# Loading Wk in quarters, two x tiles between the halves of Wq, and two blocks of Wq turned later, in a fused graph-network kernel

## The chip, the cores and the metric

One core of one Trainium2 chip runs the whole program. The metric is the device time of one execution in microseconds, taken as the median of the runs. The kernel before takes 307.28 us (three runs, all 307.28).

## What is computed

Two layers over a graph of N = 1024 nodes with D = 512 features and 16384 edges (src, dst), with dst sorted:

```
h = relu(layernorm(x))
q = h @ Wq + bq;  k = h @ Wk + bk;  v = h @ Wv + bv
a = q @ k.T / sqrt(512), masked to the pairs that are edges
x = x + softmax(a) @ v
h = relu(layernorm(x))
# degree-normalised aggregation with self loops, twice, with a batch norm and relu between
x = x + agg(relu(bn(agg(h @ W1 + b1))) @ W2 + b2)
```

The scores are not made from q and k apart. They are h (Wq Wk^T) h^T plus bias terms, so a matrix M = Wq Wk^T is made first. For it both weights are turned (transposed) on TensorE. The adjacency is a matrix of edge counts that TensorE sums up from one-hot matrices, which VectorE builds. Every float32 product is made as three passes over a high and a low part.

## The kernel before, in words

All engines run orders written out by hand and meet at semaphores. Nothing is planned at run time, so the order of the work is the order of the code.

The opening has these steps. ScalarE's queue issues the load of Wk in two halves (line 429). SyncE's queue issues the edge lists, the two halves of Wq (line 263), four tiles of x (line 243), and the two halves of Wv (line 259). TensorE first runs 26 small products on zeros.

An *item* is one block that goes through three engines: TensorE fills a bank of PSUM (`make`), ScalarE evicts the high part (`hi_of`, line 491), and VectorE subtracts it to get the low part (`lo_of`, line 688). The kinds that matter here:

- ("t", K, c) and ("t", Q, c): block c (128 rows, 256 KB) of Wk or Wq is turned with four transposes (line 1023). Below they are K0 to K3 and Q0 to Q3.
- ("m", n, 0), below m0 to m3: block n of M, twelve matmul passes (lines 989 to 991). m_n reads turned block n of Wq as its stationary side, and **all four** turned blocks of Wk.
- ("h", n, 0): a tile of normalised x is turned, and ("v", n, 0) is its product with Wv.

`start` gives each early item its bank. `nth(item)` is the item's number in the order of the list. The semaphores item_ps, item_hi and item_lo count items, so a wait for item_lo at nth(item) means that all items up to that one are done.

TensorE's order before is K0, K1, two transposes of the edge lists (bank 3), K2, K3, Q0, Q1, Q2, Q3, m0, one small transpose of `lim` into bank 0 (line 1085), m1, m2, the edge counts of window 0 (line 1055), m3, counts of window 1, h0 to h3, v0, v1, counts of window 2, and so on. m0 waits until the low part of Q0 is written, m1 for Q1, m2 for Q2 and m3 for Q3.

VectorE's order before is lo(K0), lo(K1), copies of the edge columns (lines 755 and 756, `ecol_ready`), lo(K2), lo(K3), lo(Q0), lo(Q1), `limits()` (seven small steps, lines 654 to 662, ending in `lim_ready`), lo(Q2), the read of the turned `lim` (line 762, `bounds_ready`), a load of a bound into a register, lo(Q3), `onehots(0)` (lines 705 and 707), the next bound, the low part of half of Wv (line 673), `onehots(1)`, and so on. The ring of one-hots has four places, so VectorE can be at most four groups ahead of TensorE.

ScalarE's order before is hi of K0 to Q3, `stats(0)` (sums of x tiles 0 and 1), hi(m0), half of Wv, `stats(2)`, hi(m1) and so on.

Of the kernel before, what the change touches and what calls it, by code (L numbers as in the profile page):

```python
# [17 lines left out]
P = 128  # L18
# [4 lines left out]
KC = D // P  # L23
NCH = E // P
HALF = 512
WIN = 64
NW = N // WIN
# [9 lines left out]
LOADS = 2  # L37
WARM = 26
XT = 4
# [19 lines left out]
def gnn_kernel(nc, x, src, dst, Wq, bq, Wk, bk, Wv, bv, W1, b1, gamma, beta, W2, b2, out):  # L59
# [14 lines left out]
    def hold(name, kib):  # L74
# [86 lines left out]
    ident_zeroed ident_ready zeros_ready pad_ready iota_ready tables_ready consts  # L161
    dst_in src_in ext_ready ext_ps edge_f_ready ecol_ps ecol_ready drel_ready lim_ready lim_ps bounds_ready
    x_in0 x_in1 x_in2 x_in3 qk_bias_in bcol_in bias_in b1_in
    Wk_in0 Wk_in1 Wq_in0 Wq_in1 wB_in0 wB_in1 w2_in0 w2_in1 w_hi w_lo
    x_sums x_means x_squares ln_scale ln_coef h_ready item_ps item_hi item_lo uw_ready hw_second fill_ready
    ncol_ready lead_cols lead_dist lead_made onehots onehots_used c_done c16 loops_added adj_in0 adj_in1 adj_in2 adj_in3
    deg_ready degm_ready degm_ps flag_ready dinv_ready
# [8 lines left out]


    K, Q = 0, 1
    start = {("t", K, 0): 4, ("t", K, 1): 5, ("t", K, 2): 6, ("t", K, 3): 7, ("t", Q, 0): 2, ("t", Q, 1): 3,
             ("t", Q, 2): 4, ("t", Q, 3): 5, ("m", 0, 0): 6, ("m", 1, 0): 7, ("m", 2, 0): 2, ("m", 3, 0): 3,  # L180
             ("h", 0, 0): 4, ("h", 1, 0): 5, ("h", 2, 0): 6, ("h", 3, 0): 7}
    ahead = [[], [], [("v", 0, 0), ("v", 1, 0)], [("v", 2, 0), ("h", 4, 0)], [("v", 3, 0), ("h", 5, 0)],
# [2 lines left out]
    final = {("q", 1, c): 4 + c for c in range(KC)}  # L185
    items = list(start) + sum(ahead, []) + list(final)
    nth = lambda item: items.index(item) + 1
    item_bank = lambda item: start.get(item, final.get(item, 2 + (items.index(item) - len(start)) % ITEM_BANKS))
    last_in = lambda b, end: max([n for n, other in enumerate(items[:end], 1) if item_bank(other) == b] + [0])

# [41 lines left out]
    @block.sync  # L232
    def _(sp):

        sp.dma_start(edge_i[:, 0, :], dst.rearrange("(c j) -> c j", j=P)).then_inc(S["dst_in"], 16)
        sp.dma_start(edge_i[:, 1, :], src.rearrange("(c j) -> c j", j=P)).then_inc(S["src_in"], 16)

        def load_x(n):
            if XT <= n < NT + XT:
                sp.wait_ge(S["h_ready"], n - XT + 1)  # L240
            if n >= NT + XT:
                sp.wait_ge(S["x1_ready"], n - NT - XT + 1)
            sp.dma_start(xt[:, n % XT, :], x[(n % NT) * P:(n % NT + 1) * P, :]).then_inc(S[f"x_in{n % XT}"], 16)

        def turn_counts(t):

            if t == 0:
                sp.wait_ge(S["c16"], 2 * NW)
            if t >= ADJ:
                sp.wait_ge(S["masked"], t - ADJ + 1)  # L250
            sp.dma_start_transpose(adj[:, t % ADJ, :].rearrange("p (b n) -> p b n", b=NT),
                                   cnt16[:, t, :, :].rearrange("p b n -> p (b n)")).then_inc(
                S[f"adj_in{t % ADJ}"], 16)

        def load_w(i):

            k = KC // LOADS
            for j in range(LOADS):
                sp.dma_start(weight_load(i, j, "raw"), weights[i][0].rearrange("(k p) n -> p k n", p=P)[
                    :, j * k:(j + 1) * k, :]).then_inc(S[f"{weights[i][3]}{j}"], 16)  # L260

        for j in range(LOADS):
            sp.dma_start(half_of_qk(Q, j), half_in_dram(Wq, j)).then_inc(S[f"Wq_in{j}"], 16)
        for t in range(XT):
            load_x(t)
        load_w(0)
        for t in range(XT, NT):
            load_x(t)
        for i, b in ((K, bq), (Q, bk)):
            sp.dma_start(bias_row[:, i, :], b.rearrange("(o n) -> o n", o=1).to_broadcast([P, D])).then_inc(S["qk_bias_in"], 16)  # L270
        for i, b in enumerate((gamma, beta)):
            sp.dma_start(bcol[:, i, :], b.rearrange("(c p) -> p c", p=P),
                         allow_slow_non_contiguous=True).then_inc(S["bcol_in"], 16)
        for t in range(XT):
            load_x(NT + t)
        sp.wait_ge(S["item_ps"], nth(("v", NT - 1, 0)))
        load_w(1)
        sp.wait_ge(S["uw_ready"], 4)
        sp.dma_start(bias_row[:, 0, :], bv.rearrange("(o n) -> o n", o=1).to_broadcast([P, D])).then_inc(S["bias_in"], 16)
        sp.dma_start(bias_row[:, 1, :], b1.rearrange("(o n) -> o n", o=1).to_broadcast([P, D])).then_inc(S["b1_in"], 16)  # L280
        def turn_p(t, part, split, done, landed):

            sp.wait_ge(S[split], t + 1)
            if t >= 1:
                sp.wait_ge(S[done], t)
            sp.dma_start_transpose(p16T[:, part, :, :], p16[:, part, :]).then_inc(S[landed], 16)

        def turn_h2(t, part, split, done, landed):

            sp.wait_ge(S[split], t + 1)  # L290
            if t >= 1:
                sp.wait_ge(S[done], t)
            sp.dma_start_transpose(h16T[:, part, :, :], h16[:, part, :]).then_inc(S[landed], 16)

        for t in range(ADJ):
            turn_counts(t)
        for t in range(NT + 1):
            if t < NT:
                turn_p(t, 0, "p16_hi", "p_hi", "p16_hi_in")
                turn_p(t, 1, "p16_lo", "p_lo", "p16_lo_in")  # L300
            if XT <= t + 3 < NT:
                load_x(NT + t + 3)
            if t == 0:
                load_w(2)
            if t + ADJ < NT:
                turn_counts(t + ADJ)
            if t >= 1:
                turn_h2(t - 1, 0, "h16_hi", "h2T_hi", "h16_hi_in")
                turn_h2(t - 1, 1, "h16_lo", "h2T_lo", "h16_lo_in")
        sp.wait_ge(S["xb_ready"], NT)  # L310
        sp.dma_start(bias_row[:, 0, :], b2.rearrange("(o n) -> o n", o=1).to_broadcast([P, D])).then_inc(S["bias_in"], 16)
        for t in range(NT):
            sp.wait_ge(S["out_ready"], t + 1)
            sp.dma_start(out[t * P:(t + 1) * P, :], xt[:, t % XT, :]).then_inc(S[f"out_done{t % XT}"], 16)
        for u in range(XT):
            sp.wait_ge(S[f"out_done{u}"], 16 * NT // XT)
# [108 lines left out]

    @block.scalar
    def _(act):
        for j in range(LOADS):
            act.dma_start(half_of_qk(K, j), half_in_dram(Wk, j)).then_inc(S[f"Wk_in{j}"], 16)

        def split_w(i, loads=range(LOADS)):

# [5 lines left out]
        def stats(t):  # L438

            if t == KC:  # L440
                act.wait_ge(S["item_ps"], nth(("m", KC - 1, 0)))
            for u in (t, t + 1):
                act.wait_ge(S[f"x_in{u % XT}"], 16 * (u // XT + 1))
                act.activation(row_of(u), xt[:, u % XT, :], ACT.Copy, accum_out=xsum[:, 0, u:u + 1]).then_inc(S["x_sums"], 1)
            act.wait_ge(S["x_sums"], t + 2)
            act.activation(lnc[:, 0, t:t + 2], xsum[:, 0, t:t + 2], ACT.Copy, scale=-1.0 / D).then_inc(S["x_means"], 2)
            act.wait_ge(S["x_means"], t + 2)
            for u in (t, t + 1):
                act.activation(row_of(u), xt[:, u % XT, :], ACT.Square, bias=lnc[:, 0, u:u + 1],
                               accum_out=xsum[:, 1, u:u + 1]).then_inc(S["x_squares"], 1)  # L450
# [28 lines left out]
        def hi_of(item):  # L479

            what, n, c = item
            act.wait_ge(S["item_ps"], nth(item))
            if what == "q":
                if item == ("q", 0, 0):
                    act.wait_ge(S["uw_ready"], 4)
# [12 lines left out]
            act.activation(T[:, t % 2, :], zerob[:, 0:1].to_broadcast([P, N]), ACT.Identity,  # L498
                           bias=fill[:, t:t + 1]).then_inc(S["mask_set"], 1)

        for item in list(start)[:8]:
            hi_of(item)
        stats(0)
        hi_of(("m", 0, 0))
        split_w(0, (0,))
        stats(2)
# [121 lines left out]
    def _(dve):  # L628
# [67 lines left out]
        def bounds_of(i):  # L696
            return dve.value_load(lohi[0:1, ORDER[i]:ORDER[i] + 1], min_val=256, max_val=257 * NCH)
# [59 lines left out]
        for item in early[2:6]:  # L757
            lo_of(item)
        limits()
        lo_of(early[6])  # L760
        dve.wait_ge(S["lim_ps"], 1)
        dve.tensor_scalar(lohi[0:1, :], bank(0)[0:1, 0:NW], float(NCH), None, ALU.add).then_inc(S["bounds_ready"], 1)
        dve.wait_ge(S["bounds_ready"], 1)
        bounds = bounds_of(0)
        lo_of(early[7])
        dve.wait_ge(S["ecol_ready"], 2)
        onehots(0, bounds)
        bounds = bounds_of(1)
        split_w(0, 0)
        onehots(1, bounds)  # L770
        bounds = bounds_of(2)
# [214 lines left out]
    def _(pe):  # L986
# [18 lines left out]
        def make(item):  # L1005
# [4 lines left out]
            if what in "htw":  # L1010
                if what == "h":
                    pe.wait_ge(S["h_ready"], n + 1)
                elif what == "t":
                    pe.wait_ge(S[f"{'Wk' if n == K else 'Wq'}_in{c // 2}"], 16)
                    if item_bank(item) == 3:
                        pe.wait_ge(S["ecol_ready"], 2)
                else:
                    pe.wait_ge(S["uw_ready"], 4)
                for k in range(KC):
# [59 lines left out]
        for a in range(2):  # L1079
            m = pe.transpose(bank(3)[:, a * P:(a + 1) * P], edge_f[:, a, :], ident[:, :])  # L1080
        m.then_inc(S["ecol_ps"], 1)
        for item in early[2:9]:
            make(item)
        pe.wait_ge(S["lim_ready"], 1)
        pe.transpose(bank(0)[:, 0:P], lim[:, 4:5].to_broadcast([P, P]), ident[:, :]).then_inc(S["lim_ps"], 1)
        for item in early[9:11]:
            make(item)
        pe.wait_ge(S["consts"], 1)
        pe.wait_ge(S["bounds_ready"], 1)
# [186 lines left out]
```

## Time and profile before

| | us |
|---|---|
| median of the runs | 307.28 |
| the profiled execution | 307.32 |
| its span | 305.5 |
| TensorE busy (matmul) | 295.5 (97%) |
| VectorE busy | 207.0 (68%) |
| ScalarE busy | 159.9 (52%) |

The span is what the profile covers; 1.8 us of the execution's time lie around it. The stretch that the change touches is the first 20 us. There the transposes of the weights, their evictions, the loads and the small steps on the edge lists run side by side. In the timeline each line gives a start, a length, the engine, the line of the kernel, the tile written and the tiles read, and in brackets how long the engine had been idle and who ended that.

### The profile page before, as it was taken

What the parts mean: (1) busy time and instruction counts of PE and PEld (TensorE: products, weight loads), DVE (VectorE), ACT (ScalarE), POOL (GpSimd) and SP (SyncE); (2) the same over time, 40 slices, a digit from 0 to 9 for tenths busy, and PEclk for the clock granted to TensorE, in tenths of its full rate; (3) what the DMA queues carried; (4) which work ended last, traced back from release to release, by engine and by line L of the source; (5) the groups of instructions that cost most, each with busy time, mean ns of one, the idle gap of its engine ahead of it and who ended that gap; (6) DMA issues with size and microseconds to landing.
All of it is one profiled execution on the core that took longest, in us unless ns stands there. A gap on an engine that the chain in (4) does not pass through costs nothing.

```text
span 305.5 us, 4845 instructions
## 1 busy us (share of the span) xinstructions
PE 295.5 (97%) x1345; PEld 227.3 (74%) x1345; DVE 207.0 (68%) x458; ACT 159.9 (52%) x266; POOL 57.6 (19%) x103
## 2 busy tenths in 40 slices
PE   7999889899999999999999999999999999999995
PEld 6777356466665888888888888887888888878884
DVE  3899999999977557965748575568344388276311
ACT  3999967989546546445444544357523044342000
POOL 5361353000000530032131420203010044100000
PEclk9999999999999999999999999999999999999999
DMA  7806040000600309444362625313102000000321
GB/s 256 311 23 186 1 141 0 1 0 2 207 0 3 69 3 238 79 95 89 85 148 43 150 40 104 67 38 69 34 20 52 0 3 0 0 2 0 111 98 69
DMA packets 42312, 21.67 MB, mean 71 GB/s; under 512 B 35760, under 2 KB 36016, under 8 KB 42288
## 3 DMA queue, kind: packets, MB, share of 16 engines
q1 hardware_dynamic: 41744, 20.33, 26.0%
q10 hardware_dynamic: 544, 1.05, 0.9%
q8 instruction: 12, 0.20, 0.3%
q14 instruction: 12, 0.10, 0.1%
HBM read 10.88 MB, written 2.10 MB: 42 GB/s over the span
## 4 chain that ended last, share of the span: by engine, by line
PE 86%; DVE 7%; issue 2%; DMA 1%; DVEq 1%; ACT 1%; ACTq 0%
PE ps L989 20%; PE ps L991 19%; PE ps L990 19%; PE ps L1242 10%; PE ps L1165 8%; PE ps L1055 8%; DVE src_oh L705 2%; DMA qk_raw<-L_gnn_Wk_in 1%; PE ps L1023 1%; DVE dst_oh L707 1%; DVEq L705 1%; DVE WT L688 1%; DVE T L809 0%; DVE smx L813 0%; DVE p L821 0%
## 5 line engine op out<-in xcount | busy, mean ns | idle before, releaser
L705 DVE TENSOR_SCALAR src_oh<-iota,ecol 128x512 f16 x135 | 40.0, 349 | 3.0 <-PE ps L1055 2.5
L1055 PE MATMUL ps<-src_oh,dst_oh 128*128 x135 | 34.0, 382 | 3.7 <-DVE dst_oh L707 3.3
L1165 PE MATMUL ps<-cnt,qh 128*128 128x512 f32 x128 | 30.1, 391 | 0.3 <-ACT cnt L575 0.3
L1055 PEld LDWEIGHTS ps<-src_oh,dst_oh 128*128 x135 | 13.3, 103 | 21.9 <-issue 12.5
L1242 PE MATMUL ps<-qh,cnt 128*128 128x512 f32 x128 | 29.3, 390 | 0.0
L1165 PEld LDWEIGHTS ps<-cnt,qh 128*128 128x128 f32 x128 | 23.9, 188 | 5.6 <-DVE qh L868 0.7
L1242 PEld LDWEIGHTS ps<-qh,cnt 128*128 128x128 f32 x128 | 24.0, 188 | 5.3 <-DVE vb L970 0.3
L991 PE MATMUL ps<-v,pT 128*128 128x512 f32 x64 | 25.0, 390 | 0.0
L989 PE MATMUL ps<-v,pT 128*128 128x512 f32 x64 | 24.9, 389 | 0.0
L989 PE MATMUL ps<-hT,qh 128*128 128x512 f32 x64 | 24.9, 389 | 0.0
L990 PE MATMUL ps<-v,pT 128*128 128x512 f32 x64 | 24.9, 389 | 0.0
L990 PE MATMUL ps<-hT,qh 128*128 128x512 f32 x64 | 24.9, 389 | 0.0
L991 PE MATMUL ps<-hT,qh 128*128 128x512 f32 x64 | 24.9, 389 | 0.0
L403 POOL TENSOR_SCALAR lnb<-bnag 128x1 f32<-128x1 f32 x8 | 7.2, 898 | 81.6 <-DVE bnag L842 81.6
L464 ACT ACTIVATE cnt<-ps 64x512 int16<-64x512 f32 x32 | 18.9, 590 | 6.0 <-PE ps L1072 5.4
L982 DVE SCALAR_TENSOR_TENSOR xt<-ps,dinv,x 128x512 f32<-128x512 f32 x8 | 5.7, 747 | 17.1 <-PE ps L1242 17.1
L531 ACT ACTIVATE T<-T,smx 128x1024 f32<-128x1024 f32 x8 | 9.2, 1154 | 13.9 <-DVE smx L814 13.9
L831 DVE TENSOR_SCALAR pT<-p16T 128x1024 fp32r<-128x1024 f16 x8 | 5.5, 693 | 15.6 <-DMA p16T<-p 15.5
L559 ACT ACTIVATE hnT<-h16T 128x512 fp32r<-128x512 f16 x8 | 5.1, 632 | 20.2 <-DMA h16T<-h 20.2
L809 DVE COPY_PREDICATED T<-adj,ps 128x1024 f32<-128x1024 int16 x8 | 10.6, 1321 | 7.4 <-PE ps L991 7.4
L498 ACT ACTIVATE T<-zerob,fill 128x1024 f32<-128x1024 bf16 x8 | 9.1, 1146 | 12.4 <-DVE p L821 12.4
L707 DVE TENSOR_TENSOR dst_oh<-iota_w,drel_first 128x384 f16 (+1 forms) x35 | 14.7, 421 | 0.6 <-PE ps L1055 0.6
(186 smaller groups left out, 685.2 us busy)
## 6 DMA issues: line engine op xcount, KB each, us to landing
xt<-x_in SPq DMA_DIRECT2D x16, 256.0 KB, 3.3
out<-xt SPq DMA_DIRECT2D x8, 256.0 KB, 2.1
qk_raw<-L_gnn_Wk_in ACTq DMA_DIRECT2D x2, 512.0 KB, 5.0
qk_raw<-L_gnn_Wq_in SPq DMA_DIRECT2D x2, 512.0 KB, 6.8
wB_raw<-L_gnn_Wv_in SPq DMA_DIRECT2D x2, 512.0 KB, 9.0
wB_raw<-L_gnn_W_in SPq DMA_DIRECT2D x2, 512.0 KB, 4.1
w_raw<-L_gnn_W_in SPq DMA_DIRECT2D x2, 512.0 KB, 4.6
bias_row<-L_gnn_b_in SPq DMA_DIRECT2D x2, 256.0 KB, 4.7
```

The source lines that it names most:

```text
L464: act.activation(cnt16[rows, a * KC:(a + 1) * KC, w // 2, :], ps[a * WIN:(a + 1) * WIN, i % 2, :].rearrange("p (s n) -> p s n", n=P), ACT. ...
L498: act.activation(T[:, t % 2, :], zerob[:, 0:1].to_broadcast([P, N]), ACT.Identity, bias=fill[:, t:t + 1]).then_inc(S["mask_set"], 1)
L531: act.activation(T[:, t % 2, :], T[:, t % 2, :], ACT.Exp, bias=smx[:, 1, t:t + 1], scale=SCALE, accum_out=smx[:, 2, t:t + 1]).then_inc(S[" ...
L705: dve.tensor_scalar(src_oh[:, bass.ds(slot, 1), j, :].rearrange("p a n -> p (a n)"), iota[:, :], ecol[:, bass.ds(c + j, 1)], None, ALU.is_ ...
L707: dve.tensor_tensor(dst_oh[:, bass.ds(slot, 1), :, 0:count].rearrange("p a n u -> p (a n) u"), iota_w[:, :, 0:count], drel(i)[:, bass.ds(c ...
L809: dve.copy_predicated(T[:, t % 2, :], adj[:, t % ADJ, :], ps[:, 2 * (t % 2):2 * (t % 2) + 2, :].rearrange("p a n -> p (a n)")).then_inc(S[ ...
L989: pe.matmul(out_, stat(1), mov(0), start=first, stop=False)
L990: pe.matmul(out_, stat(0), mov(1), start=False, stop=False)
L991: return pe.matmul(out_, stat(0), mov(0), start=False, stop=last)
L1055: m = pe.matmul(ps[:, i % 2, :], dst_oh[:, bass.ds(slot, 1), :, j].rearrange("p a n -> p (a n)"), lead_oh[:, i % 2, j, :] if first and ACT ...
L1165: m = pe.matmul(bank(g), qh[:, d, a, c * P:(c + 1) * P], cnt[:, d, n * HALF:(n + 1) * HALF], start=(d == 0 and a == 1), stop=last)
L1242: m = pe.matmul(bank(t), cnt[:, d, t * P:(t + 1) * P], qh[:, d, a, :], start=(d == 0 and a == 1), stop=last)
```

## The change

Wk is loaded as four quarters, one for each block, and each has a semaphore of its own. On SyncE's queue x tiles 0 and 1 are now issued behind the first half of Wq, and x tiles 2 and 3 behind the second half. Q1 gets bank 0 in place of bank 3, and the turned `lim` gets bank 3 in place of bank 0. TensorE now makes m0 behind Q1, then turns `lim`, then Q2 and Q3, then m1. ScalarE does `stats(0)` before hi(Q2) and hi(Q3). VectorE does `onehots(0)` and loads the next bound before lo(Q2) and lo(Q3). `nth_made` is the number of an item in TensorE's new order, and ScalarE's waits use it.

```diff
-    start = {("t", K, 0): 4, ("t", K, 1): 5, ("t", K, 2): 6, ("t", K, 3): 7, ("t", Q, 0): 2, ("t", Q, 1): 3,
+    start = {("t", K, 0): 4, ("t", K, 1): 5, ("t", K, 2): 6, ("t", K, 3): 7, ("t", Q, 0): 2, ("t", Q, 1): 0,
+    in_order_made = items[:6] + items[8:9] + items[6:8] + items[9:]
+    nth_made = lambda item: in_order_made.index(item) + 1
@@ sync
         for j in range(LOADS):
             sp.dma_start(half_of_qk(Q, j), half_in_dram(Wq, j)).then_inc(S[f"Wq_in{j}"], 16)
-        for t in range(XT):
-            load_x(t)
+            for t in range(2 * j, 2 * j + 2):
+                load_x(t)
@@ scalar
-        for j in range(LOADS):
-            act.dma_start(half_of_qk(K, j), half_in_dram(Wk, j)).then_inc(S[f"Wk_in{j}"], 16)
+        for c in range(KC):
+            act.dma_start(qk_raw[:, K, c, :], Wk[c * P:(c + 1) * P, :]).then_inc(S[f"Wk_in{c}"], 16)
-        for item in list(start)[:8]:
+        for item in list(start)[:6]:
             hi_of(item)
         stats(0)
+        for item in list(start)[6:8]:
+            hi_of(item)
         hi_of(("m", 0, 0))
@@ vector
         limits()
-        lo_of(early[6])
         dve.wait_ge(S["lim_ps"], 1)
-        dve.tensor_scalar(lohi[0:1, :], bank(0)[0:1, 0:NW], float(NCH), None, ALU.add).then_inc(S["bounds_ready"], 1)
+        dve.tensor_scalar(lohi[0:1, :], bank(3)[0:1, 0:NW], float(NCH), None, ALU.add).then_inc(S["bounds_ready"], 1)
         dve.wait_ge(S["bounds_ready"], 1)
         bounds = bounds_of(0)
-        lo_of(early[7])
         dve.wait_ge(S["ecol_ready"], 2)
         onehots(0, bounds)
         bounds = bounds_of(1)
+        for item in early[6:8]:
+            lo_of(item)
         split_w(0, 0)
@@ tensor
-                    pe.wait_ge(S[f"{'Wk' if n == K else 'Wq'}_in{c // 2}"], 16)
-                    if item_bank(item) == 3:
-                        pe.wait_ge(S["ecol_ready"], 2)
+                    pe.wait_ge(S[f"Wk_in{c}" if n == K else f"Wq_in{c // 2}"], 16)
-        for item in early[2:9]:
+        for item in early[2:6] + early[8:9]:
             make(item)
+        pe.wait_ge(S["ecol_ready"], 2)
         pe.wait_ge(S["lim_ready"], 1)
-        pe.transpose(bank(0)[:, 0:P], lim[:, 4:5].to_broadcast([P, P]), ident[:, :]).then_inc(S["lim_ps"], 1)
-        for item in early[9:11]:
+        pe.transpose(bank(3)[:, 0:P], lim[:, 4:5].to_broadcast([P, P]), ident[:, :]).then_inc(S["lim_ps"], 1)
+        for item in early[6:8] + early[9:11]:
             make(item)
```

## Rows read from the trace of the kernel before

**Rows 1.** The page: shares of the chain that ended last, by engine.

```profile
PE 86%; DVE 7%; issue 2%; DMA 1%; DVEq 1%; ACT 1%; ACTq 0%
```

**Rows 2.** Timeline, TensorE, 8 to 19 us: start, length, engine, line, tiles, count.

```profile
8.04 1.09 PE L1023 MATMUL ps<-ident,qk_raw 128*128 128x128 f32 x8 [0.19 <-DMA qk_raw<-L_gnn_Wq_in]
...
9.48 1.07 PE L1023 MATMUL ps<-ident,qk_raw 128*128 128x128 f32 x8 [0.34 <-DVE WT L688]
...
10.30 0.48 PE L989 MATMUL ps<-WT 128*128 128x512 f32 x1
...
13.14 0.27 PE L1085 MATMUL ps<-ident,lim 128*128 128x128 f32 x1
...
13.16 0.48 PE L989 MATMUL ps<-WT 128*128 128x512 f32 x1
...
15.99 0.39 PE L989 MATMUL ps<-WT 128*128 128x512 f32 x1
...
18.72 1.26 PE L1055 MATMUL ps<-src_oh,dst_oh 128*128 x5
```

**Rows 3.** Timeline, ScalarE and VectorE, 8 to 18 us, same columns.

```profile
8.19 2.47 DVE L688 TENSOR_TENSOR WT<-ps,WT 128x512 fp32r<-128x512 f32 x4
...
8.73 1.09 ACT L491 ACTIVATE WT<-ps 128x512 fp32r<-128x512 f32 x2 [0.20 <-PE ps L1023]
...
10.59 0.34 DVE L654 TENSOR_SCALAR hit<-ps,win 128x128 f32<-128x128 f32 x1
...
13.44 0.16 DVE L762 TENSOR_SCALAR lohi<-ps 1x16 int32<-1x16 f32 x1
...
14.56 0.69 DVE L688 TENSOR_TENSOR WT<-ps,WT 128x512 fp32r<-128x512 f32 x1 [0.95 <-DVE lohi L762]
...
15.16 0.60 DVE L705 TENSOR_SCALAR src_oh<-iota,ecol 128x512 f16 x2
...
17.42 1.23 DVE L673 TENSOR_TENSOR wB<-wB_raw,wB 128x1024 fp32r<-128x1024 f32 x1 [0.20 <-issue]
```

**Rows 4.** Timeline: the issues of the loads on both queues.

```profile
0.72 0.98 ACTq L429 DMA_DIRECT2D qk_raw<-L_gnn_Wk_in  x2
...
1.65 0.94 SPq L263 DMA_DIRECT2D qk_raw<-L_gnn_Wq_in  x2
...
2.63 2.12 SPq L243 DMA_DIRECT2D xt<-x_in  x4
```

**Rows 5.** DMA view, short windows: each load, KB, us from issue to landing.

```profile
qk_raw<-L_gnn_Wk_in ACTq DMA_DIRECT2D x1, 512.0 KB, 4.4
...
qk_raw<-L_gnn_Wk_in ACTq DMA_DIRECT2D x1, 512.0 KB, 5.5
qk_raw<-L_gnn_Wq_in SPq DMA_DIRECT2D x1, 512.0 KB, 6.3
edge_i<-src_in SPq DMA_DIRECT2D x1, 64.0 KB, 4.1
...
qk_raw<-L_gnn_Wq_in SPq DMA_DIRECT2D x1, 512.0 KB, 7.2
xt<-x_in SPq DMA_DIRECT2D x1, 256.0 KB, 7.4
```

**Rows 6.** DMA view, 4.5 to 5.0 us: queue, packets, MB, share (q10 ScalarE's, q1 SyncE's).

```profile
q10 hardware_dynamic: 91, 0.18, 92.7%
q1 hardware_dynamic: 57, 0.03, 17.4%
```

**Rows 7.** Timeline, 25 to 33 us: TensorE at v0, VectorE with its ring full.

```profile
25.88 0.47 PE L989 MATMUL ps<-wB,hT 128*128 128x512 f32 x1 [0.15 <-DVE hT L688]
...
32.31 0.90 DVE L705 TENSOR_SCALAR src_oh<-iota,ecol 128x512 f16 x3 [0.59 <-PE ps L1055]
```

**Rows 8.** The chain of waits in order of time: start, length, what released the next step.

```profile
25.79 0.09 issue
```

**Rows 9.** Waits, 0 to 50 us: who waited for whom, total, times, longest.

```profile
PE ps L1055 <- DVE dst_oh L707: 2.3, 7, 0.4
```

More of the change, by code:

```diff
@@ L163, in gnn_kernel @@
     x_in0 x_in1 x_in2 x_in3 qk_bias_in bcol_in bias_in b1_in
-    Wk_in0 Wk_in1 Wq_in0 Wq_in1 wB_in0 wB_in1 w2_in0 w2_in1 w_hi w_lo
+    Wk_in0 Wk_in1 Wk_in2 Wk_in3 Wq_in0 Wq_in1 wB_in0 wB_in1 w2_in0 w2_in1 w_hi w_lo
     x_sums x_means x_squares ln_scale ln_coef h_ready item_ps item_hi item_lo uw_ready hw_second fill_ready
@@ L440, in stats @@
             if t == KC:
-                act.wait_ge(S["item_ps"], nth(("m", KC - 1, 0)))
+                act.wait_ge(S["item_ps"], nth_made(("m", KC - 1, 0)))
             for u in (t, t + 1):
@@ L481, in hi_of @@
             what, n, c = item
-            act.wait_ge(S["item_ps"], nth(item))
+            act.wait_ge(S["item_ps"], nth_made(item))
             if what == "q":
```

## The prediction

> **What bounds the kernel now.** I read the page first. TensorE carries 86% of the chain that ended last [rows 1], so the question at each place is whether TensorE stands still or has more in front of it. Then I read the timeline of the opening, because the change touches nothing else. From 10.30 us on TensorE runs without a gap: m0 starts at 10.30, the small transpose of the bounds is at 13.14, m1 starts at 13.16, m2 at 15.99, and the first edge counts at 18.72 [rows 2]. A product of twelve passes takes 2.83 us (15.99 - 13.16), or 2.86 with the small transpose before it (13.16 - 10.30). Before 10.30 there are gaps, and in them TensorE waits for data: the eight transposes of Q0 and Q1 start at 8.04 behind a load, and those of Q2 and Q3 at 9.48 [rows 2]. So the opening is paced by loads up to about 10 us and by TensorE's own work after that.
>
> When do the loads land? Issue plus time to landing [rows 4, 5] gives: first half of Wk 0.72 + 4.4 = 5.12; the src list 5.29 (issue 1.19, between Wk's halves, + 4.1); second half of Wk 1.21 + 5.5 = 6.7; Wq's halves 1.65 + 6.3 = 7.95 and 2.12 + 7.2 = 9.32; x tile 0 2.63 + 7.4 = 10.03. Halves come 1.25 to 1.6 us apart and the 256 KB tile 0.7 us behind the last half. The engines are full, and they serve the loads close to the order of issue, whichever queue they come from: at 4.5 to 5.0 us ScalarE's queue moved 0.18 MB and SyncE's 0.03 MB [rows 6], although Wq had been issued since 1.65.
>
> Which wait let m0 start at 10.30? Not Wq's arithmetic. The four low parts K2, K3, Q0, Q1 start at 8.19 and last 2.47 together [rows 3]; each is 0.68 (one alone took 0.69 at 14.56), so they start 0.60 apart, so Q0's ends near 10.07, and with 0.09 for the handover (from the end of a low part of h at 25.79 to v0 at 25.88 [rows 7, 8]) m0 could have started at 10.16. It started when the transposes of Q2 and Q3 were out of its way: 10.30 - 9.48 = 0.82 us for eight of them [rows 2]. They filled a gap that ran from about 9.1 to 10.16 in any case.
>
> **The change part by part.**
>
> *Q2 and Q3 behind m0.* This frees at most 10.30 - 10.16 = 0.14 us ahead of m0. It adds eight transposes between m0 and m1, where TensorE had no gap: +0.82 us by the distance just read, at most 1.07 by their busy time [rows 2]. I take 0.82, since it is start to start. Cover that stood over them is gone.
>
> *Wk in quarters.* The bytes ahead of m0 stay the same: it needs all of Wk and the first half of Wq, and the last of these landed at 7.95. Quarters can only change which of them is last. Two halves cost 0.98 us to issue, 0.49 each [rows 4]. The trace has no quarter of Wk; an x tile of the same size took 2.12 / 4 = 0.53. With 0.45 to 0.5 each, the four start near 0.72, 1.2, 1.7 and 2.2. SyncE issues the first half of Wq at 1.65 and x tile 0 now at 2.12. So by order of issue the third quarter is level with Wq's first half and the fourth falls behind it. K3 then lands at 7.95 in place of 6.7, and Q0 with it or shortly before. The first quarter lands about 0.65 earlier, but K0's low part waits in VectorE's line behind the edge steps, so this gains nothing at m0. ScalarE is held by its two added issues for 1 us, before any eviction: cost nothing.
>
> The chain to m0 is then: transposes from 8.04; hi(K3) from 8.73, the 0.69 us that Q0 took from its transposes to its eviction [rows 2, 3]; it lasts about 0.6, since two overlapping ones take 1.09, so lo(K3) from 9.34, lo(Q0) 0.60 later from 9.94 to 10.62, m0 at 10.71. lo(Q1) runs 10.54 to 11.22. m0 comes 0.41 later than before instead of earlier. The bounds are: if all of Wk is served ahead of Wq, Q0 alone decides, lo(Q0) ends at 10.02 and m0 starts at 10.11, so 0.60 less; if the fourth quarter falls behind x tile 0 as well, it lands 0.68 later and everything with it.
>
> *x tiles between Wq's halves.* Wq's second half lands some 1.35 us later, near 10.7. Q2 is turned after 13, so it costs nothing. x tiles 0 and 1 land before ScalarE wants them. Hidden too, on both sides.
>
> *ScalarE's order.* stats(0) stood behind the evictions of Q2 and Q3 and now starts two evictions (1.09 us [rows 3]) earlier against them, while Q2 itself is in its bank only past 14. hi(Q2) is not late by it. hi(m0) moves back by the time of those two evictions, and nobody waits for it before h2 needs the bank. Zero; if Q2's eviction were late after all, VectorE is busy with one-hots until 17.1 and hides up to 2 us of it.
>
> *VectorE's order.* This is the second cost. m2 waits for lo(Q2), and lo(Q2) now stands behind the bounds and the one-hots of window 0. `limits` started 0.60 behind the start of lo(Q1) and ended at 12.80, which is 2.21 after its start at 10.59 [rows 3]. Now it starts at 11.15 and ends at 13.36. TensorE's bounds transpose follows at 13.45 (m0's last pass is issued at 10.71 + 2.61 = 13.32, so it doesn't wait for that). lohi comes 0.30 after it (13.44 - 13.14 [rows 2, 3]), at 13.75. From lohi to VectorE's next instruction there were 14.56 - 13.44 = 1.12 us, the load of a bound into the register [rows 3]; one-hots from 14.87. They and the next load took 17.42 - 15.16 = 2.26 [rows 3], so lo(Q2) runs 17.13 to 17.81 and m2 may start at 17.90. TensorE would be there earlier: 13.45 + 0.10 + 0.82 + 2.83 = 17.20. So it stands still for 0.70. Queued behind that wait are the counts of window 0, m3, window 1 and all of h.
>
> *Banks.* Q1 no longer waits for the edge columns, but the eight transposes at 8.04 run in one piece [rows 2], so that wait cost nothing. The new wait for them in front of `lim` is long past. Zero.
>
> **Sum.** m2 starts at 17.90 in place of 15.99: +1.91 us. It has three terms against a start of m0 at 10.30: +0.41 (loads), +0.82 (transposes, of which with the handovers 0.80 is left), +0.70 (the wait for lo(Q2)). Is it given back later? Up to v0 TensorE has one gap, 0.15 at 25.88 [rows 7], and that is a wait for its own transposes to be evicted. In the counts after 31.5 us TensorE waits for VectorE (2.3 us in seven waits [rows 8]), which could absorb a delay if VectorE kept its old times. It doesn't: VectorE reaches those one-hots behind the low parts of h0 to h3, which TensorE makes, and at 32.31 it had itself waited 0.59 for TensorE with its ring full [rows 7]. So both move together. The profiled execution took 307.32 us, 0.04 above the median of the runs. 307.32 + 1.91 = 309.2.
>
> **A rule weighed.** Rows 6 show SyncE's queue at a sixth of the bytes of ScalarE's while both have work. The Trainium skill (DMA: Bandwidth & Descriptors, Queues, rings and completion order) says that each engine takes turns between the queues it has work for, packet by packet. Whether the first half of Wq was yet visible to the engines at that time isn't shown, so the rule isn't refuted; it is the last rival below.
>
> **The rivals.**
>
> - *Wk served first.* ScalarE's quarters are issued fast enough to stay ahead of Wq. m0 at 10.11, its bounds transpose behind the last pass at 12.95, lohi 13.25, one-hots 14.37, lo(Q2) to 17.31, m2 at 17.40: +1.4, 308.7 us. For it: issue times are nearly level. Chance 0.20.
> - *The fourth quarter behind x tile 0.* +0.68 on the sum: 309.9. For it: x tile 0 moves to 2.12, about where the quarter stands. Chance 0.18.
> - *Equal turns between the queues.* Wk's 1 MB would be through only when SyncE's queue had moved as much, the edge lists, half of Wq and an x tile and a half, near 9.0 by the landings above: 1.05 later than 7.95, so +2.96, 310.3. Against it stand rows 6 and the landing of Wk at 6.7. Chance 0.04.
> - *Absorbed.* TensorE's waits for one-hots [rows 9] take up 1.4 of the 1.91 us, because VectorE keeps its old times: 307.8. It would need VectorE's low parts of h0 to h3 not to move, and they follow TensorE. The same time comes out if Wk is served first and lo(Q2) isn't late (m2 at 10.11 + 2.86 + 0.82 + 2.83 = 16.62, +0.63: 307.95). Chance 0.07.
> - *Faster.* The smaller first loads let the DMA engines reach their full rate sooner, and the whole train lands earlier. Each us earlier takes one off m2. The place is K3 and Q0, the point from which it decides 7.95 - 1.91 = 6.04 us: both would have to be there before that, which only just was the time of the second half of Wk. At 5.7 it would give 307.0. Against it: the bytes are the same and the halves come at a steady pace. Chance 0.06.
>
> **How the numbers follow.** The forecast has 0.45, the other three on its side 0.42 together. A measurement of this kernel can tell about 0.2% from no change, 0.6 us. Slower by more than that is 0.87, within it 0.07, faster 0.06. The range goes from 308.0 (just above the first rival without the wait for lo(Q2)) to 310.3 (equal turns). What lies outside are the last two cases and a tail.
>
> **What would show it.** In the profile after, TensorE's first pass of m0 at 10.7 (10.1 if Wk is served first, 11.4 if behind x); the eight transposes of Q2 and Q3 just after the bounds transpose; m2 at 17.9, with a wait of 0.7 us for VectorE's low part in front; lohi at 13.75; the counts of window 0 at 20.6 in place of 18.72; v0 at 27.8 in place of 25.88; and the same distance from there to the end. The prediction is wrong if m0 starts before 9.5, if m2 doesn't wait, or if the distance from v0 to the end shrinks.

## The result: slower by 1.2%

The changed kernel takes 310.9 us (median of five runs, 310.42 to 313.95), against 307.28 for the kernel before (five runs here, 307.17 to 308.27): a ratio of 1.0122, interval 1.0092 to 1.0151. The forecast was 309.2 with a range up to 310.3. The direction was right, the size too small, and the measured time lies above the range.

The times of both kernels fall on two levels, and no number below can be read without them. The kernel before takes 307.0 to 307.9, mostly below 307.6, or 308.0 and more, mostly up to 308.8. The changed kernel mostly takes 310.4 to 311.2, and now and then 313.6 to 314.0. Its first profile is of a run of the upper level (313.95, span 312.1). The second profile is of a run of 310.45, span 308.6, which is of the lower level, where most runs lie, and 0.45 below the median. It is read first.

TensorE's timeline of the second profile, columns as in [rows 2]:

```profile
8.54 1.53 PE L1025 MATMUL ps<-ident,qk_raw 128*128 128x128 f32 x12 [1.23 <-DMA qk_raw<-L_gnn_Wk_in]
11.30 0.47 PE L993 MATMUL ps<-WT 128*128 128x512 f32 x1 [1.23 <-DVE WT L692]
...
14.13 0.27 PE L1088 MATMUL ps<-ident,lim 128*128 128x128 f32 x1
14.24 1.04 PE L1025 MATMUL ps<-ident,qk_raw 128*128 128x128 f32 x8
15.04 0.47 PE L993 MATMUL ps<-WT 128*128 128x512 f32 x1
...
19.22 0.47 PE L993 MATMUL ps<-WT 128*128 128x512 f32 x1 [1.18 <-DVE WT L692]
...
22.07 1.26 PE L1057 MATMUL ps<-src_oh,dst_oh 128*128 x5
...
27.13 1.95 PE L1025 MATMUL ps<-ident,T 128*128 128x128 f32 x16
```

K3, Q0 and Q1 are turned at 8.54, behind 1.23 us of waiting for a quarter of Wk. m0 starts at 11.30 (10.30 before), m1 at 15.04 (13.16), m2 at 19.22 (15.99), and the first counts at 22.07 (18.72) [rows 2]. Three waits of 1.2 us stand in front of K3, m0 and m2. The transposes of h start at 27.13. Those of the kernel before start at 23.78, so 3.35 us have been lost by then, and the whole span (what the profile covers) is longer by 3.1 (308.6 against 305.5).

VectorE's timeline of the same profile, to be held against [rows 3]:

```profile
11.66 0.34 DVE L658 TENSOR_SCALAR hit<-ps,win 128x128 f32<-128x128 f32 x1
...
14.44 0.16 DVE L765 TENSOR_SCALAR lohi<-ps 1x16 int32<-1x16 f32 x1 [0.56 <-PE ps L1088]
16.11 0.62 DVE L709 TENSOR_SCALAR src_oh<-iota,ecol 128x512 f16 x2 [1.51 <-issue]
...
18.38 1.29 DVE L692 TENSOR_TENSOR WT<-ps,WT 128x512 fp32r<-128x512 f32 x2 [0.20 <-issue]
```

lohi is ready at 14.44 and the one-hots start 1.67 us later, with nothing between them. The low part of Q2 starts at 18.38, and m2 waits for it.

The DMA view of the same profile (issue at 1.65 for Wq, 2.12 for x tile 0 and about 2.1 for the fourth quarter; the last column is us from issue to landing):

```profile
qk_raw<-L_gnn_Wq_in SPq DMA_DIRECT2D x1, 512.0 KB, 5.2
...
xt<-x_in SPq DMA_DIRECT2D x1, 256.0 KB, 6.0
qk_raw<-L_gnn_Wk_in ACTq DMA_DIRECT2D x1, 256.0 KB, 6.4
```

Wq's first half lands at 6.85, x tile 0 at 8.1, the fourth quarter of Wk at 8.5. Before, Wk was complete at 6.7 and Wq's half came at 7.95 [rows 4, 5]. The order has turned round.

How the two queues share the DMA engines shows in their packets (queue, packets, MB, share; q10 is ScalarE's with Wk, q1 SyncE's). The kernel before from 4.5 to 5.0 us, all packets of both queues (the queues apart are [rows 6]), and from 5.5 to 6.0:

```profile
DMA packets 148, 0.21 MB, mean 411 GB/s; under 512 B 11, under 2 KB 60, under 8 KB 148
...
q10 hardware_dynamic: 58, 0.10, 53.4%
q1 hardware_dynamic: 50, 0.10, 52.5%
```

The second profile of the changed kernel from 4.5 to 5.0:

```profile
DMA packets 99, 0.20 MB, mean 406 GB/s; under 512 B 0, under 2 KB 0, under 8 KB 99
## 3 DMA queue, kind: packets, MB, share of 16 engines
q1 hardware_dynamic: 56, 0.11, 59.2%
q10 hardware_dynamic: 43, 0.09, 45.7%
```

In the kernel before SyncE's 57 packets of [rows 6] are still the edge lists, at most 512 B each, beside 91 of mostly 2 KB for Wk. That is a sixth of the bytes, but more than half as many packets. Its first packet of Wq starts only at 5.2, when four fifths of Wk are through. In the changed kernel it starts at 3.8 (4.4 in the first profile), and from there the quarters of Wk have to share the engines with Wq.

The first profile, of the upper level, shows the same picture and one thing more. The page's shares of the chain, and TensorE's timeline:

```profile
PE 74%; DVE 7%; ACT 6%; issue 4%; DMA 4%; POOL 2%; DVEq 2%; POOLq 1%; ACTq 0%
```

```profile
9.39 2.82 PE L1025 MATMUL ps<-ident,qk_raw 128*128 128x128 f32 x12 [0.83 <-DMA qk_raw<-L_gnn_Wk_in]
12.86 0.77 PE L993 MATMUL ps<-WT 128*128 128x512 f32 x1 [0.65 <-DVE WT L692]
...
15.56 0.63 PE L993 MATMUL ps<-WT 128*128 128x512 f32 x1
15.98 0.63 PE L994 MATMUL ps<-WT 128*128 128x512 f32 x1
...
17.25 0.40 PE L994 MATMUL ps<-WT 128*128 128x512 f32 x1
17.48 0.39 PE L995 MATMUL ps<-WT 128*128 128x512 f32 x1
17.71 0.27 PE L1088 MATMUL ps<-ident,lim 128*128 128x128 f32 x1
...
22.79 0.47 PE L993 MATMUL ps<-WT 128*128 128x512 f32 x1 [1.19 <-DVE WT L692]
```

Ten of m0's twelve passes follow each other at 0.43 us instead of 0.23, and twelve transposes take 2.82 us instead of 1.53. A pass of 512 columns in 0.43 us is TensorE's lower level, 1.2 GHz (512 / 0.43 us); 0.23 us is near what 2.4 GHz gives. From 17.25 on it is at the upper one. The granted clock in the profile (the third number from the end of this line for 13 to 17 us, 1.00) says full speed all through these 17 us, so here the spacing shows what that column does not:

```profile
13.00:17.00 4.00, 4.00 (x10) 3.13 (x11) 2.49 (x8) 2.79 (x9) 0.92 (x2) 1.00 0.16 58
```

m0 starts 1.56 us later than in the second profile (12.86 against 11.30) and takes 4.85 us instead of 2.83. Together that is 3.6, and the spans differ by 3.5. Of the 1.56 us, 0.85 come from a load and not from the clock: the fourth quarter landed at 9.3 in place of 8.5, and K3 is turned from 9.39 in place of 8.54.

### The profile page after: what moved, and what is told of

It reads as the page before. It is cut to its first block, busy times and chain, and to the rows that moved or that the text cites. A ratio compares the mean times of both kernels' runs of the same rounds, so it can differ in the third digit from the quotient of the medians.

```text
span 312.1 us, 4840 instructions
## 1 busy us (share of the span) xinstructions
PE 298.9 (96%) x1339; PEld 231.3 (74%) x1345; DVE 207.4 (66%) x458; ACT 160.4 (51%) x266; POOL 58.6 (19%) x103
## 4 chain that ended last, share of the span: by engine, by line
PE 74%; DVE 7%; ACT 6%; issue 4%; DMA 4%; POOL 2%; DVEq 2%; POOLq 1%; ACTq 0%
PE ps L993 17%; PE ps L995 16%; PE ps L994 16%; PE ps L1245 9%; PE ps L1168 8%; PE ps L1057 5%; DMA qk_raw<-L_gnn_Wk_in 2%; DMA p16T<-p 2%; DVE src_oh L709 1%; POOL drel_second L367 1%; ACT hrow L451 1%; POOLq L371 1%; DVE T L813 1%; ACT hrow L446 1%; PE ps L1025 1%
## 5 line engine op out<-in xcount | busy, mean ns | idle before, releaser
L1057 PE MATMUL ps<-src_oh,dst_oh 128*128 x131 | 33.0, 381 | 4.1 <-DVE dst_oh L711 3.0
```

The source lines that it names most:

```text
L1057: m = pe.matmul(ps[:, i % 2, :], dst_oh[:, bass.ds(slot, 1), :, j].rearrange("p a n -> p (a n)"), lead_oh[:, i % 2, j, :] if first and ACT ...
```

## The experiments

**The parts, each by itself.** Four kernels shared the runs of the kernel before (median 308.03 there, because half of its 21 runs fell in its upper level). The changed kernel once more:

> The changed kernel once more. In its first profile TensorE ran the transposes from 5.4 us and m0 at 0.43 us a pass instead of 0.23, and m2 started 6.8 us later than before, though the median of its runs is only 3.6 us above. Theory 1 (the rate of TensorE in the opening differs from run to run): here m0 may run at 0.23 us a pass; then the span is near 308.7 to 309.3 and m2 starts 3 to 4 us late. Theory 2 (the loads alone make the loss): m0 has 0.43 us a pass again, K3 lands near 9.3 again, and the time is the same as in the first profile.

310.75 us (310.45 to 313.64), ratio 1.0125 (1.0068 to 1.0182). m0 at 0.23 us a pass, span 308.6, m2 3.2 us late: theory 1. This is the second profile of above.

**Only the order** (order_only below). The loads are put back, the new order of all engines stays:

```diff
+        for j in range(LOADS):
+            act.dma_start(half_of_qk(K, j), half_in_dram(Wk, j)).then_inc(S[f"Wk_in{j}"], 16)
...
-            for t in range(2 * j, 2 * j + 2):
-                load_x(t)
+        for t in range(XT):
+            load_x(t)
```

> The new order on all engines, but the loads as in the kernel before (Wk in halves, x tiles behind Wq). My sum of before without the load term: m0 at 10.1, m2 at 17.4 with a wait for the low part of Q2, +1.4 us, 308.7. Load theory in its pure form: near 0. If the rate of TensorE is what went, it stays at 0.23 us a pass here, since the loads come as before.

309.51 us, ratio 1.0064 (1.0042 to 1.0085); most runs at 309.2 to 309.55, two at 310.7. TensorE's and VectorE's lines:

```profile
10.05 0.47 PE L993 MATMUL ps<-WT 128*128 128x512 f32 x1 [1.10 <-DVE WT L692]
...
13.77 0.47 PE L993 MATMUL ps<-WT 128*128 128x512 f32 x1
...
17.96 0.47 PE L993 MATMUL ps<-WT 128*128 128x512 f32 x1 [1.18 <-DVE WT L692]
...
25.87 1.95 PE L1025 MATMUL ps<-ident,T 128*128 128x128 f32 x16
```

```profile
13.18 0.16 DVE L765 TENSOR_SCALAR lohi<-ps 1x16 int32<-1x16 f32 x1 [0.54 <-PE ps L1088]
14.85 0.61 DVE L709 TENSOR_SCALAR src_oh<-iota,ecol 128x512 f16 x2 [1.51 <-issue]
```

This is the case "Wk served first" of the prediction, and it can be laid beside it step by step: m0 forecast at 10.11 and found at 10.05, lohi 13.25 and 13.18, one-hots 14.37 and 14.85, m2 17.40 and 17.96. One term is off by half a us, the step from lohi to the one-hots. The rest holds. h is turned 2.09 us later than before, and the span is 1.9 longer (307.4).

**Halves, with x between** (halves). Only Wk's loads are put back:

> The changed kernel with Wk in halves again; x tiles stay between the halves of Wq. If the quarters are the load term: K3 back at 6.7, the time as order_only, near +1.4. If the x tiles are it: as the changed kernel, +3.6.

309.77 us, ratio 1.0073 (1.0048 to 1.0097). That can't be told from order_only, the run above. The x tiles are not the load term; the quarters are.

**Only the quarters.** The kernel before with four quarters on ScalarE's queue:

> The kernel before with Wk in quarters, nothing else changed. Load theory: the fourth quarter queues behind half of Wq and lands near 8.6 to 9.3 instead of 6.7; K3, Q0, Q1 follow it, Q2 and Q3 after them, m0 starts near 11.5, so +1 to +1.5 us. If quarters slow TensorE's rate as well, +3 or more. Order theory (the loss is the order of m0, Q2, Q3 and the one-hots): within 0.4 us of the kernel before.

308.44 us (308.15 to 309.03), ratio 1.0015 (1.0001 to 1.0029) against runs of both levels, and 1.1 us above the lower one. Against the mean of all 21 runs beside it (307.99) its mean is 0.5 above. The fourth quarter takes 7.0 us from its issue near 2.1, so 9.1:

```profile
7.72 0.66 PE L1023 MATMUL ps<-ident,qk_raw 128*128 128x128 f32 x4 [1.70 <-DMA qk_raw<-L_gnn_Wk_in]
9.15 2.40 PE L1023 MATMUL ps<-ident,qk_raw 128*128 128x128 f32 x20 [0.77 <-DMA qk_raw<-L_gnn_Wk_in]
11.90 0.47 PE L989 MATMUL ps<-WT 128*128 128x512 f32 x1 [0.36 <-DVE WT L688]
```

TensorE waits 2.5 us for quarters, m0 starts 1.6 us late, and the span is 1.4 longer (306.9). So the quarters, meant to come sooner, cost more than a us against the lower level. The two parts add up: 1.9 (order) and 1.4 (quarters) make 3.3, and both together have 3.1.

**Why the fourth quarter is late.** All quarters on SyncE's queue, ahead of Wq:

```diff
-        for c in range(KC):
-            act.dma_start(qk_raw[:, K, c, :], Wk[c * P:(c + 1) * P, :]).then_inc(S[f"Wk_in{c}"], 16)
...
+        for c in range(KC):
+            sp.dma_start(qk_raw[:, K, c, :], Wk[c * P:(c + 1) * P, :]).then_inc(S[f"Wk_in{c}"], 16)
         for j in range(LOADS):
             sp.dma_start(half_of_qk(Q, j), half_in_dram(Wq, j)).then_inc(S[f"Wq_in{j}"], 16)
```

> The changed kernel with the quarters of Wk issued on SyncE's queue ahead of Wq instead of on ScalarE's. In the changed kernel the fourth quarter was issued at 2.1 and landed at 8.5 to 9.3, behind all of Wq's first half, issued at 1.65, and about with x tile 0. Theory (loads are served close to the order of issue, and 256 KB pieces on ScalarE's queue share with what SyncE has issued): here all quarters are ahead of Wq, the fourth lands by 7.2, Wq's half near 8.5, m0 starts near 10.6, and the time is that of the halves, about 309.8. Rival (a quarter is slow in itself): the fourth quarter still lands after 8.5, time 310.7 or more.

310.82 us, ratio 1.0121 (1.0089 to 1.0154). The DMA view has the fourth quarter (issued at 3.1) and the half of Wq (issued at 3.54):

```profile
qk_raw<-L_gnn_Wk_in SPq DMA_DIRECT2D x1, 256.0 KB, 3.8
...
qk_raw<-L_gnn_Wq_in SPq DMA_DIRECT2D x1, 512.0 KB, 5.3
```

The quarter now lands at 6.9, so a quarter isn't slow in itself. It has no second queue to share the engines with here, and all of Wq is behind it; the run doesn't tell these two apart. The time didn't follow, though: the half of Wq lands at 8.84, later than before (7.95), and m0 starts at 11.05. In this kernel the loads moved 272 GB/s from 4 to 5 us and 338 from 7 to 8, against 399 and 385 in the kernel before. The first part of my theory, an early quarter, is shown. Its last part, the time, was wrong: 310.82 is what the rival had, though not by its mechanism. One queue didn't keep the engines full.

The packets show where the time of a late quarter goes. In all nine profiles with Wk in halves on ScalarE's queue, Wq's first packet starts at 5.0 to 5.3 us and Wk's last one at 6.0 to 6.8. In all seven with quarters on that queue, Wq's first packet starts at 3.8 to 4.4 and Wk's last one at 7.8 to 8.9; the fourth quarter lands at 8.2 to 9.3. The small packets of the edge lists, which stand ahead of Wq on SyncE's queue, get through sooner beside quarters. Why they do is open.

**The wait for the low part of Q2** (lo_first). The kernel is order_only with the two low parts ahead of the one-hots:

```diff
         bounds = bounds_of(0)
+        for item in early[6:8]:
+            lo_of(item)
         dve.wait_ge(S["ecol_ready"], 2)
         onehots(0, bounds)
         bounds = bounds_of(1)
-        for item in early[6:8]:
-            lo_of(item)
```

> The new order with the loads as before (as order_only), but VectorE does the low parts of Q2 and Q3 before the one-hots of window 0. In order_only the bounds were ready at 13.18, one-hots started 1.67 us later although nothing stood between, and m2 waited 1.18 us for the low part of Q2. Theory: that gap of 1.67 us is the fetch of the bound into the register and can hold both low parts, so they are free, the wait at m2 goes, m2 starts near 16.8 instead of 17.96, and the time falls by 1.2 us to 308.3. Rival (the gap is a fixed price after each register load and comes again): the low parts push the one-hots back by 1.3 us and the counts of window 0 wait for them; then the time falls by less than 0.5.

308.32 us, ratio 1.0026 (1.0006 to 1.0046), as the theory had it: 1.2 us below order_only. VectorE's lines:

```profile
13.73 0.16 DVE L765 TENSOR_SCALAR lohi<-ps 1x16 int32<-1x16 f32 x1 [0.57 <-PE ps L1088]
14.84 1.29 DVE L692 TENSOR_TENSOR WT<-ps,WT 128x512 fp32r<-128x512 f32 x2 [0.95 <-ACT WT L493]
16.05 0.60 DVE L709 TENSOR_SCALAR src_oh<-iota,ecol 128x512 f16 x2
```

From lohi to the one-hots are 2.32 us with both low parts, 1.21 us of work, between them. Without them it was 1.67, so the two cost 0.65 there and m2 has no wait left. m2 starts at 17.17 and not near 16.8, because m0 started at 10.57 in this run (10.05 in order_only); from m0 to m2 are 6.60 us in place of 7.91.

**The upper level.** Four kernels change the number of products on zeros at the start, and one fills the gaps of the changed kernel. The kernel before with 32 and with 18 in place of 26:

```diff
-WARM = 26
+WARM = 32
```

> The kernel before with 32 instead of 26 products on zeros. It has two levels as well, 307.0 to 307.6 and 308.2 to 308.8. Theory (gap behind the zero products): only the lower one is left, median 307.3, ratio near 0.998. Rival: both levels, median between them.

> The kernel before with 32 products on zeros once more. Theory: again a single level near 307.25, none of the runs at 308.1 or above, ratio 0.997 to 0.999. Rival (chance in the first ten runs): both levels, ratio 1.

307.26 us (307.13 to 307.65) with ratio 0.9973 (0.9960 to 0.9986), and again 307.34 (307.02 to 308.08) with 0.9988 (0.9973 to 1.0002). One of 22 runs is at 308.0 or above. Of the 86 runs of the unchanged kernel before, made beside the experiments, 38 were. So six more products on zeros all but remove the upper level of the kernel before.

> The kernel before with 18 products on zeros instead of 26, so that TensorE stands still from 3.0 to 4.4 us. Theory: the transposes from 5 us and perhaps m0 run at half rate (0.23 us a transpose pair, 0.43 us a pass of m0) in most runs, and the time is 1 to 4 us higher. Rival: within 0.3 us of the kernel before.

308.28 us (307.82 to 310.17), ratio 1.0016 (0.9993 to 1.0039). In its profile TensorE stood still for 1.55 us, eight transposes at 5.37 took 1.97, and m0 ran at 0.23 us a pass from 11.06. The lower level near 307.3 is gone and the mean is hardly moved: less than the theory wanted.

> The kernel before once more, to see which of its two levels a profile falls in and what differs. If at 308.2 or above: the transposes between 5 and 7.5 us run at half rate (eight in 1.9 instead of 1.1 us) and m0 starts about 1.2 us later than 10.3. If at 307.3: as the first profile.

307.44 us (307.09 to 308.48), both levels; the profile was of the lower one. So no profile of the upper level of the kernel before exists, and what differs in it stays unseen.

The changed kernel with 34 products, and with 18:

> The changed kernel with 34 instead of 26 products on zeros ahead of the first transpose, so that TensorE has no gap between 3.9 and 4.8 us. The changed kernel has two levels, 310.4 to 310.9 and 313.6 to 314.0, and the profile of the higher one shows TensorE at half its rate until 16.8. Theory (the gap behind the zero products decides the level): the higher level is gone and no run is above 311.5. Rival (the level has nothing to do with that gap): both levels are seen again.

> The changed kernel with 18 products on zeros in place of 26. Theory (its higher level is TensorE's rate not having risen before the gaps in front of K3 and m0): with less work ahead the rate rises late more often, so half of the runs or more are above 312.5. Rival (the level is set by something outside TensorE's work): about one run in four, as with 26.

With 34: 310.2, 310.63, 310.63 and 313.38. The upper level is still there, so the gap right behind the zero products does not decide it; that theory fell. With 18: three runs at 310.7 to 310.9, one at 312.2, two at 313.4 to 313.5. Two of six above 312.5 is less than the half or more that the theory wanted, and not far from the one in four of the rival, so these runs decide nothing. The profile (310.89) even speaks against the theory: four transposes ahead of the gap at K3 took 1.06 us, the lower level, and the twelve behind it, with 0.81 us of waiting and nothing filled in, took 1.54, the upper one.

Then the gaps in front of K3 and m0 were filled:

```diff
         for item in early[2:6] + early[8:9]:
+            if item == early[8]:
+                pe.wait_ge(S["ecol_ready"], 2)
+            if item in (early[3], early[8]):
+                for _ in range(8):
+                    pe.matmul(bank(7 if item == early[3] else 3)[:, 0:P], zerob[:, :], zerob[:, :], start=True, stop=True)
             make(item)
```

> The changed kernel with eight products on zeros put into each of its two gaps, before K3 and before m0 (16 more products in free banks, their results unused). Theory (the changed kernel's higher level at 313.6 to 314.0 comes when TensorE's rate hasn't risen before these gaps, which keep it low until m0 has run): with the gaps filled the higher level is gone or falls below 312, the lower stays at 310.4 to 310.9. Rival (the level is set before, by the start of the run): still runs above 313.

> The changed kernel with both gaps filled once more, for more runs. Theory: again none above 312, the rest near 310.8. Rival: one in four above 313.

310.81 us (310.54 to 311.39) and 310.74 (310.5 to 311.54). None of twelve runs is above 311.6, while two of nine of the changed kernel were above 313. TensorE's lines in the first of the two:

```profile
7.17 1.06 PE L1025 MATMUL ps<-ident,qk_raw 128*128 128x128 f32 x4
8.03 1.06 PE L1089 MATMUL ps<-zerob 128*128 128x128 bf16 x8
...
11.77 0.47 PE L993 MATMUL ps<-WT 128*128 128x512 f32 x1 [0.79 <-DVE WT L692]
12.54 0.39 PE L993 MATMUL ps<-WT 128*128 128x512 f32 x1
```

The transposes at 7.17 and the fill still run at the lower level, and m0 runs at the upper one. That agrees with the theory that the two waits, which the change itself brought, can leave TensorE at 1.2 GHz until m0 is nearly done. The profile with 18 products shows that the first of these waits does not always do so. With these counts of runs the cause of the upper level is not shown.

**What m0 first is worth.** lo_first with 32 products, against the kernel before with 32:

> The new order with the loads as before, the low parts of Q2 and Q3 ahead of the one-hots, and 32 products on zeros. Against the kernel before with 32 products (307.26, a single level) only the place of m0 ahead of Q2 and Q3 is left. By my sum m0 starts 0.25 earlier and eight transposes cost 0.8 behind it, so +0.6: 307.9, single level. If m0 first is worth something by itself, below 307.3.

308.11 us (307.81 to 308.93), against 307.26 and 307.34: +0.8. m0 starts at 10.38 and m2 at 16.95 without a wait. The forecast was +0.6. The place of m0 ahead of Q2 and Q3 is a loss even without the quarters and the late low parts. ScalarE's new order and the banks are in this difference too; they were not run alone.

## Why the prediction was off

Span and start of h in each profile, against the kernel before (305.5 and 23.78):

| kernel | h turned later by | span longer by |
|---|---|---|
| lo_first | 1.18 | 1.2 |
| quarters only | 1.60 | 1.4 |
| order only | 2.09 | 1.9 |
| halves | 2.49 | 2.2 |
| changed, second profile | 3.35 | 3.1 |
| changed, first profile | 6.93 | 6.6 |

- *What bounds the kernel, and whether a delay is given back.* Right. Whatever is lost before h is turned is lost at the end, but for 0.0 to 0.3 us. The rival "absorbed" is out.
- *Eight transposes on TensorE's path, 0.82 us.* Right: from the small transpose to m1 are 0.91 us (15.04 - 14.13) where there were 0.02 [rows 2].
- *The loads, +0.41 at m0.* This step failed first. "They serve the loads close to the order of issue, whichever queue they come from" put the fourth quarter level with Wq's half, at 7.95. It came at 8.5 and 9.3 in the two profiles, and m0 started at 11.30 where the forecast had 10.71. Wq's half, which came at 7.95 before, was here at 6.85, and the fourth quarter, issued half a us behind it, landed 1.65 behind it; in order of issue its 256 KB would have been some 0.7 behind, the distance of x tile 0 from the half ahead of it in the kernel before (10.03 - 9.32 [rows 4, 5]). The step rests on [rows 6], read by bytes. By packets the queues were not far apart there, 91 to 57, and where both move packets of 2 KB they share the engines about evenly: 58 to 50 in the kernel before from 5.5 to 6.0 us, 43 to 56 in the changed one from 4.5 to 5.0. The shares are not even in every stretch; from 5 to 6 us of the first profile SyncE's queue had 166 packets and ScalarE's 34. The Trainium skill (DMA: Bandwidth & Descriptors, Queues, rings and completion order) says that an engine takes turns between queues packet by packet; the packets of most stretches here agree. Wk complete at 6.7 in the kernel before is no case against it, since no packet of Wq moved before 5.2. So the rival "equal turns between the queues", with a chance of 0.04, had the mechanism nearest to what the packets show; its landing near 9.0 lies within the 8.2 to 9.3 of the profiles. That quarters let Wq start sooner was in no part of the forecast.
- *The wait for the low part of Q2, 0.70 us.* The wait is there, with 1.18 us. The second failed step is "from lohi to VectorE's next instruction there were 1.12 us", which put the one-hots at 14.87. I took the next instruction for the one-hots. It was the low part of Q3, which fits into the time that the fetch of the bound takes in any case. The one-hots stood 1.72 us behind lohi before (15.16 - 13.44 [rows 3]) and 1.67 now. Moving Q3's low part out of there freed 0.05 us, not 0.60. That is a row that I had, misread.
- *Banks, ScalarE's order, x tiles:* nothing, as forecast, for the x tiles: halves and order_only can't be told apart. Banks and ScalarE's order were not run alone.
- *The upper level.* Not foreseen. It isn't in the median, and adds 3 us to about a fifth of the runs (two of nine). Its cause stays open.

Sum for the second profile: m2 was forecast at 17.90 and started at 19.22. Of the 1.32, 0.59 is m0's start and 0.55 the step behind lohi. About 0.1 is the small transpose, which had to wait for m0's last pass, and the rest is small steps. The run of this profile took 310.45, and the median of the five is 310.9; what makes up this 0.45 is not known. The rival "fourth quarter behind x tile 0" has m0 at 11.4 and with the corrected step gives 309.9 + 0.55 = 310.45, the time of this run. That is luck in part: it took the loads in order of issue too, and in the profile with 34 products the quarter landed at 8.2, ahead of Wq's half at 8.7. The sum of the forecast cites [rows 8] for the seven waits of 2.3 us; they are [rows 9], and nothing hangs on it.

The better of both is the kernel before with 32 products on zeros: 307.3, with the upper level nearly gone. The best of the new order (lo_first) stays 0.26% above the kernel before.

## What to carry to other kernels

Work that fills a wait costs nothing where it stands, and its full length on the critical path: eight transposes and a low part were both moved out of such a place. Cutting a load into pieces doesn't only let the first piece come early. Here the *last* piece came 1.5 to 2.6 us later, because another queue's load began to move sooner and shared the engines with it. So ask when the last piece that the consumer needs will land. And read the share of two queues by packets as well as by bytes: 57 small packets and 91 large ones look like one queue being served first. When a profile shows a gap of "issue" around a small instruction, ask whether the instruction fills the gap or makes it, before it is priced.

## What was not expected of the hardware

The way Wk was cut on ScalarE's queue changed when SyncE's queue got to its first packet of Wq: at 5.0 to 5.3 us with halves, at 3.8 to 4.4 with quarters, in all 16 profiles.

A value read from a tile into VectorE's register held back the instruction that needs it for 1.67 us behind the write (1.51 of them idle), while an instruction that doesn't need it could run 1.1 us behind it. That the fetch is the cause is inferred from the order of the instructions and from lo_first; the profile calls the gap "issue".

A single queue with 256 KB pieces did not fill the DMA engines: 272 to 375 GB/s from 4 to 9 us, against 385 to 401 where both queues issued halves.

TensorE's passes ran at the 1.2 GHz spacing, 0.43 us, until 17 us in one run and at 0.23 in the next of the same kernel, with a granted clock of 1.00 shown in both.
